# Constants of the graph convolution made inside its first layer instead of in a stage of their own

## The chip, the cores and the metric

One core of a Trainium2 chip runs one program. The metric is device microseconds from launch to end, and the median of several runs is what counts. The engines are TensorE (PE), VectorE (DVE), ScalarE (ACT), GpSimd (POOL) and SyncE (SP, which here only issues DMAs).

## The reference

`x` is 6250 nodes by 768, with 100000 edges plus a self loop for each node.

```python
x = x + gnn(_layernorm(x))        # two GCN layers, relu between them
x = x + ffn(_layernorm(x)[None])  # soft mixture of 32 experts with 32 slots each
# one GCN layer:  out = segment_sum((h @ W)[src] * dinv[src] * dinv[dst], dst) + b
# in the ffn:     phin = scale * phi / max(sqrt(sum(phi * phi, axis=0)), 1e-12)   (phi: 768 x 1024)
```

## The kernel before

The program runs five stages, each a block in which every engine has its own instruction list, with a barrier between them: `prepare` (layer norm, degrees, index tables, and a table of the node rows as a high and a low fp16 half in HBM), `constants`, `first_layer`, `second_layer` and `mixture`. All products are made with numbers split into two fp16 halves, so that a product takes three matmul passes (high by high, high by low, low by high).

`constants` loads W1, b1, W2, b2 and phi, finds power-of-two scales for W1 and W2 (largest absolute value, over the partitions by `partition_all_reduce` on POOL), computes a bound on the layer's output from sums of squares, splits W1 and W2 into halves (`W1s`, `W2s`), and normalises the columns of phi: squares, a sum over the rows by matmuls with ones, root, reciprocal, product, and again two halves (`phi_h`, `phi_l`).

`first_layer` goes over 49 blocks of 128 destination nodes. For each block POOL issues 17 indirect gathers of 128 rows (3072 bytes a row) into a ring of 17 buffers. It may run at most 17 gathers ahead of what PE has consumed (`consumed`). PE multiplies each gathered tile by a one-hot matrix (`pick`, made by DVE in `choose`) and sums in PSUM (`a_part`, L1021). The rest of a block is a chain over PE, DVE and ACT, laid between the sum steps of the next block: DVE adds the block's own rows and evicts the sum (L965, L967), ACT and DVE make its halves `v2`, PE turns them (L1009), ACT and DVE copy the turned halves to `vT` (L928, L984), PE multiplies by W1 (L1002), DVE and ACT make the hidden halves (L987 to L992), PE turns these, ACT and DVE copy them (L934, L994), PE multiplies by W2, ACT and DVE write the result's halves (L924, L975), and SP stores them. The engines take their work strictly in the order of the code, in which PE's loop reads

```python
if i >= 2: product(W2s)    # block i - 2
steps(0, 5);  turn(v2)     # block i - 1
steps(5, 9);  product(W1s) # block i - 1
steps(9, 14); turn(h2)     # block i - 1
steps(14, CT)
```

and DVE's, for block i: evict; low half of `v2`; low half of the stage of block i-1; `choose(i + 2)`; `add_own_rows(i + 1)` (L952, L954); copy to `vT` (L984); then bias, relu and halves, and the second copy.

## Time and the profile before

| | us |
|---|---|
| median of 3 runs | 3570.77 |
| lowest, highest | 3568.49, 3575.01 |
| the profiled execution, whole | 3575.02 |
| its span, first to last instruction | 3573.1 |
| PE busy in it | 3145.4 (88%) |
| DVE, ACT, POOL busy | 2003.8, 1196.0, 1860.2 |

The mean granted TensorE clock of the profiled execution is 0.972 of full speed. DMA moved 1016.48 MB, 284 GB/s on average. Times in the trace are microseconds from the start of its span. In a timeline row, the time in brackets is how long the engine was idle before the row, and what ended it.

### The profile page before, as it was taken

Reading aid. Unit: us, or ns where it says so; the run is one execution under the profiler, and the core shown is the slowest. Engines: PE = TensorE matmul, PEld = TensorE weight load, DVE = VectorE, ACT = ScalarE, POOL = GpSimd, SP = SyncE. Lnnn points to the kernel's source line nnn. Section 1 sums busy time; section 2 is a strip of 40 time slices with the busy share of each in tenths; the row PEclk is TensorE's granted clock in tenths of the full one; section 3 lists DMA queues with packets and bytes.
Section 4 is the critical chain, followed back from the end, with each engine's and each line's share of the span. In section 5 each row is a group of like instructions: output and inputs, shape, how many; then the busy total and the mean of one; then the engine's idle time right before and its main releaser. Section 6 shows DMA issues by size and latency. Waiting matters only on the chain. (4 is left out here: it accounts for less than half of the span.)

```text
span 3573.1 us, 60435 instructions
## 1 busy us (share of the span) xinstructions
PE 3145.4 (88%) x19503; PEld 2021.5 (57%) x19503; DVE 2003.8 (56%) x3053; ACT 1196.0 (33%) x1434; POOL 1860.2 (52%) x1757
## 2 busy tenths in 40 slices
PE   7214999999999999969999999999999985579998
PEld 6202666666666666635666666666666652235555
DVE  7865444444444444438888788887887872102422
ACT  6762222222222222215444444444444440111000
POOL 0104777777777777557666666666666620210000
PEclk9997999999999999989999999999999997789999
DMA  9374999999988999669888888888888848978975
GB/s 374 127 272 147 326 325 307 313 308 305 311 309 304 312 309 308 222 241 350 295 306 297 299 302 299 305 300 295 308 299 305 301 172 343 329 250 242 331 185 142
DMA packets 343943, 1016.48 MB, mean 284 GB/s; under 512 B 145058, under 2 KB 148924, under 8 KB 335472
## 3 DMA queue, kind: packets, MB, share of 16 engines
q0 software_dynamic: 139360, 696.24, 56.6%
q1 hardware_dynamic: 193252, 286.28, 23.9%
q10 hardware_dynamic: 11052, 30.21, 2.5%
q8 instruction: 179, 2.93, 0.3%
q14 instruction: 100, 0.82, 0.1%
HBM read 852.96 MB, written 133.90 MB: 276 GB/s over the span
## 5 line engine op out<-in xcount | busy, mean ns | idle before, releaser
L1194 POOL DMA_INDIRECT rows_mem<-table,idx x833 | 923.4, 1109 | 474.2 <-PE m_part L1373 235.3
L898 POOL DMA_INDIRECT rows_mem<-table,idx x833 | 883.1, 1060 | 347.2 <-issue 178.8
L1021 PE MATMUL a_part<-rows_mem,sums_mem 128*128 128x512 f16 (+1 forms) x3332 | 581.7, 328 | 48.1 <-DMA rows_mem<-table,idx 43.7
L1373 PE MATMUL m_part<-rows_mem,sums_mem 128*128 128x512 f16 (+1 forms) x3332 | 598.5, 329 | 28.7 <-DMA rows_mem<-table,idx 23.2
L1373 PEld LDWEIGHTS m_part<-rows_mem,sums_mem 128*128 128x128 f16 x3332 | 422.2, 142 | 171.2 <-issue 41.5
L1021 PEld LDWEIGHTS a_part<-rows_mem,sums_mem 128*128 128x128 f16 x3332 | 414.3, 142 | 176.7 <-issue 57.9
L1388 PE MATMUL m_ps_s<-m_dw,m_xn 128*128 128x512 f16 x1764 | 429.6, 380 | 32.3 <-DVE slots L1260 31.2
L1760 PE MATMUL e_po<-e_eh,e_cT 128*128 128x512 f16 (+1 forms) x1568 | 330.6, 331 | 67.1 <-DMA e_cT<-cw_dram 45.2
L1401 PE MATMUL m_ps_l<-phi_mem,m_xT 128*128 128x512 f16 x1764 | 388.7, 379 | 0.0
L1388 PEld LDWEIGHTS m_ps_s<-m_dw,m_xn 128*128 128x128 f16 x1764 | 210.3, 126 | 183.3 <-issue 57.8
L1401 PEld LDWEIGHTS m_ps_l<-phi_mem,m_xT 128*128 128x128 f16 x1764 | 172.5, 98 | 206.6 <-issue 0.2
L1760 PEld LDWEIGHTS e_po<-e_eh,e_cT 128*128 128x128 f16 x1568 | 152.7, 99 | 180.5 <-DMA e_cT<-cw_dram 47.8
L1002 PE MATMUL a_ps_o<-W2h,a_vT 128*128 128x512 f16 (+1 forms) x1176 | 248.4, 327 | 0.9 <-ACT a_vT L934 0.9
L1002 PE MATMUL a_ps_o<-W1h,a_vT 128*128 128x512 f16 (+1 forms) x1176 | 247.1, 326 | 2.0 <-DVE a_vT L984 2.0
L987 DVE SCALAR_TENSOR_TENSOR a_u<-a_ps_o,inv,brow 128x768 f32<-128x768 f32 x49 | 49.9, 1018 | 329.5 <-PE a_ps_o L1002 329.5
L1260 DVE TENSOR_TENSOR slots<-slots,m_ps_s 128x512 f32<-128x512 f32 x288 | 196.5, 684 | 42.4 <-PE m_ps_s L1388 41.8
L1200 ACT ACTIVATE m_part<-m_zeros 128x1536 f32<-128x1536 f32 x50 | 72.7, 1453 | 379.2 <-DVE sums_mem L1291 371.0
L1760 PE MATMUL e_po<-e_el,e_cT 128*128 128x512 f16 (+1 forms) x784 | 195.1, 331 | 0.0
L931 ACT ACTIVATE sums_mem<-a_u,dinv_s 128x768 f16<-128x768 f32 x49 | 45.9, 936 | 430.1 <-DVE a_u L987 430.1
L1002 PEld LDWEIGHTS a_ps_o<-W2h,a_vT 128*128 128x128 f16 x1176 | 115.4, 98 | 75.7 <-ACT a_vT L934 1.2
L1002 PEld LDWEIGHTS a_ps_o<-W1h,a_vT 128*128 128x128 f16 x1176 | 115.0, 98 | 76.0 <-ACT a_vT L928 2.1
L1002 PE MATMUL a_ps_o<-W2l,a_vT 128*128 128x512 f16 x588 | 144.3, 327 | 0.0
(357 smaller groups left out, 3930.1 us busy)
## 6 DMA issues: line engine op xcount, KB each, us to landing
sums_mem<-table SPq DMA_DIRECT2D x98, 384.0 KB, 6.0
rows_mem<-table,idx POOLq DMA_INDIRECT x1666, 5.2
cw_dram<-m_cst SPq DMA_DIRECT2D x49, 512.0 KB, 5.6
x_pad<-xs SPq DMA_DIRECT2D x7, 2688.0 KB, 23.9
table<-arena SPq DMA_DIRECT2D x49, 384.0 KB, 2.7
table<-a_stage SPq DMA_DIRECT2D x49, 384.0 KB, 4.2
sums_mem<-x_pad SPq DMA_DIRECT2D x49, 384.0 KB, 5.5
x_dram<-sums_mem SPq DMA_DIRECT2D x49, 384.0 KB, 4.2
```

The source lines that it names most:

```text
L898: pool.indirect_dma_start(out=ring[:, t, :], out_offset=None, in_=table, in_offset=bass.IndirectOffsetOnAxis(ap=idx[:, k:k + 1], axis=0)). ...
L931: nc.scalar.activation(h2[:, 0, :], u[:, :], ACT.Relu, scale=dinv_s2[:, bass.ds(b, 1)]).then_inc(h_hi, 1)
L987: v.scalar_tensor_tensor(u[:, :], ps_o[:, 0:D], inv[:, 0:1], brow[:, :], ALU.mult, ALU.add).then_inc(biased, 1)
L1002: mm = nc.tensor.matmul(ps_o[:, a:z], vT[:, half, c * P:(c + 1) * P], Wp[:, c, a:z], start=(c == 0 and half == 0 and Wp is Ws[0]), stop=(c ...
L1021: mm = nc.tensor.matmul(part[:, bass.ds(to + a, z - a)], pick[:, i % 2, :, t], ring[:, t, half * D + a:half * D + z], start=False, stop=(t ...
L1194: pool.indirect_dma_start(out=ring[:, t, :], out_offset=None, in_=table, in_offset=bass.IndirectOffsetOnAxis(ap=idx[:, n:n + 1], axis=0)). ...
L1200: nc.scalar.activation(part[:, :], zeros[:, :].to_broadcast([P, 3 * 512]), ACT.Copy).then_inc(wiped, 1)
L1260: v.tensor_tensor(slots[:, c, a:a + 512], slots[:, c, a:a + 512], ps_s[:, unit % 2, :], ALU.add).then_inc(added, 1)
L1373: mm = nc.tensor.matmul(part[:, bass.ds(off + at, e - f)], pick[:, i % 2, :, t], ring[:, n % RING, half * D + f:half * D + e], start=False ...
L1388: mm = nc.tensor.matmul(ps_s[:, u % 2, :], spread(xn[:, q % XN, xh, :], DC)[:, c, :], dw[:, q % DW, dh, a:a + 512], start=(q == bins[0] an ...
L1401: mm = nc.tensor.matmul(ps_l[:, a:a + 512], xT[:, half, c * P:(c + 1) * P], ph[:, c, a:a + 512], start=(c == 0 and half == 0 and ph is phi ...
L1760: mm = nc.tensor.matmul(ps_o[:, k % 2, a:e], cT[:, k % RT, half * HK + c, :], ee[:, HK * h + c, a:e], start=(c == 0 and half == 0 and ee i ...
```

## The change

`constants` and its barrier are gone, and what it did is spread over `first_layer`. The fp32 copies of W1, W2 and phi lie where they are free at that time (`slots`, `phi_mem`), and the squares of the weights in the place of W2's halves.

- SP issues W1, b1 and W2 right behind the load of block 0's own rows. phi, scale and b2 follow at its step 3, once W1's low half is made (`lo1`).
- POOL does the `partition_all_reduce` between gather 17 and gather 18.
- DVE runs `weight_scales` before block 0's eviction, `weight_halves` after it, `out_scales` in block 1, and W2's low half after block 0's copy to `vT`. ACT squares W1 and W2 and makes W1's high half before block 0, and W2's high half in it.
- The column sums of W2's squares are made by one DVE reduction over six chunks (`col_part`) and one ones-matmul, where 6 matmuls a column range did it before.
- phi's work is cut into parts of one 128x1024 chunk (a quarter of 1024 columns for the reciprocal), one part a block in `phi_parts`, on ACT and DVE from block 4 to block 29. PE gets one pair of 128x512 fp32 matmuls, at its step 12.

The core of the diff:

```diff
-                constants(nc, W1, b1, W2, b2, phi, scale, W1s, W2s, brow1, brow2, inv1, out2, dinv, dinv_s2, dinv_g,
-                          phi_h, phi_l, scl, slots, rows_mem, sums_mem, phi_mem)
...
+                    if i == 0:
+                        sp.dma_start(Wf1.rearrange("p (c d) -> p c d", c=DC), W1.rearrange("(c p) n -> p c n", p=P)).then_inc(w1_in, 16)
+                        sp.dma_start(brow[:, :], b1.rearrange("(o d) -> o d", o=1).to_broadcast([P, D])).then_inc(w1_in, 16)
+                        sp.dma_start(Wf2.rearrange("p (c d) -> p c d", c=DC), W2.rearrange("(c p) n -> p c n", p=P)).then_inc(w2_in, 16)
+                    if i == SQ_AT - 1:
+                        sp.wait_ge(lo1, 1)
+                        sp.dma_start(phi_f[:, :, :], phi.rearrange("(c p) e s -> p c (e s)", p=P)).then_inc(p_in, 16)
...
+                    if k == CT:
+                        pool.wait_ge(maxed, 2)
+                        pool.partition_all_reduce(wm[:, :], mx[:, :], P, bass.bass_isa.ReduceOp.max).then_inc(allmax, 1)
...
+                    v.tensor_reduce(u[:, :], sqw.rearrange("p (c d) -> p d c", c=DC), AX_X, ALU.add).then_inc(col_part, 1)
...
+                def weight_halves():
+                    v.wait_ge(f1_sum, 1)
+                    link(v.tensor_scalar(top2[:, :], ps_s[:, 0:1], 1.001 * D, None, ALU.mult))
+                    link(v.tensor_tensor(top2[:, :], top2[:, :], bsq[:, :], ALU.add))
+                    v.wait_ge(col_sum, 1)
+                    link(v.tensor_reduce(col[:, :], ps_o[:, 0:D], AX_X, ALU.max))
+                    link(v.scalar_tensor_tensor(top2[:, :], top2[:, :], 2.0, col[:, :], ALU.mult, ALU.mult))
+                    v.nop().then_inc(bound_r, 1)
+                    v.wait_ge(hi1, 1)
+                    v.scalar_tensor_tensor(flat(W1s[1]), Wf1, sc1[:, 0:1], flat(W1s[0]), ALU.mult, ALU.subtract).then_inc(lo1, 1)
...
+                def phi_parts(i):
+                    c = i - SQ_AT - 1
+                    if 1 <= c < DC:
+                        v.wait_ge(sqp_r, c + 1)
+                        wait(v, sqp_sum, c - 1)
+                        v.tensor_tensor(norm, norm, sq[c % 2], ALU.add).then_inc(sqp_sum, 1)
+                    if i == NORM_AT:
+                        v.wait_ge(rooted, 1)
+                        link(v.tensor_scalar(norm, norm, EPS_L2, None, ALU.max))
+                        link(v.tensor_scalar(scl[:, :], scl[:, :], 1.0 / (US * US), None, ALU.mult))
+                    c = i - RECIP_AT
+                    if 0 <= c < NR:
+                        part_n = norm[:, c * K // NR:(c + 1) * K // NR]
+                        link(v.reciprocal(part_n, part_n))
+                    c = i - UNIT_AT
+                    if 0 <= c < DC:
+                        v.tensor_tensor(phi_f[:, c, :], phi_f[:, c, :], norm, ALU.mult).then_inc(unit, 1)
+                    c = i - HIGH_AT - 1
+                    if 0 <= c < DC:
+                        v.wait_ge(unit, DC)
+                        v.wait_ge(hip, c + 1)
+                        v.scalar_tensor_tensor(phi_l[:, c, :], phi_f[:, c, :], US, phi_h[:, c, :], ALU.mult, ALU.subtract).then_inc(lop, 1)
...
                     if i + 1 < NBR:
                         add_own_rows(i + 1)
                     if i < NBR:
+                        phi_parts(i)
                         v.wait_ge(v_turned, i + 1)
                         wait(v, prod2, i)
                         v.tensor_copy(vT[:, 1, :], ps_t[:, 1, 0:D]).then_inc(vt_lo, 1)
+                        if i == 0:
+                            v.wait_ge(hi2, 1)
+                            v.scalar_tensor_tensor(flat(W2s[1]), Wf2, sc2[:, 0:1], flat(W2s[0]), ALU.mult, ALU.subtract).then_inc(lo2, 1)
```

`SQ_AT` is 4, `NORM_AT` 12, `RECIP_AT` 13, `UNIT_AT` 17 and `HIGH_AT` 23.

POOL's list, from the end of `prepare`, before the change (L728 is the reduction over the partitions, L898 a gather):

```order
L725 UNCONDITIONAL_BRANCH
L728 ISA
L728 ISA k_wm<-k_mx 128x2
L714 UNCONDITIONAL_BRANCH
L73 ISA
L893 UNCONDITIONAL_BRANCH
L898 DMA rows_mem<-table,idx 128x1536 x833
```

and with the change (L800 the reduction, L803 a gather):

```order
L795 UNCONDITIONAL_BRANCH
L803 DMA rows_mem<-table,idx 128x1536 x17
L800 ISA
L800 ISA a_wm<-a_mx 128x2
L803 DMA rows_mem<-table,idx 128x1536 x816
L769 UNCONDITIONAL_BRANCH
```

The reduction moved from its own stage to a place between two gathers.

DVE's list for block 0, from the low half of `v2` (L970) to the bias (L987), before the change:

```order
L970 SCALAR_TENSOR_TENSOR sums_mem<-sums_mem,dinv_as 128x768
L939 TENSOR_TENSOR sums_mem<-iota_x,dloc 128x2304
L820 TENSOR_LOAD tab
L820 ISA x2
L952 ISA
L952 TENSOR_TENSOR a_base<-sums_mem 128x768
L954 TENSOR_TENSOR a_base<-a_base,sums_mem 128x768
L984 COPY a_vT<-a_ps_t 128x768
L987 SCALAR_TENSOR_TENSOR a_u<-a_ps_o,inv,brow 128x768
```

and with the change, without the same five rows between L876 and L954 (L971 is the low half of `v2`, L908 and L993 the low halves of W1 and W2, L990 the copy, L996 the bias):

```order
L971 SCALAR_TENSOR_TENSOR sums_mem<-sums_mem,dinv_as 128x768
L901 TENSOR_SCALAR a_top<-a_ps_t 128x1
L902 TENSOR_TENSOR a_top<-a_top,a_bsq 128x1
L904 TENSOR_REDUCE a_col<-a_ps_o 128x1
L905 SCALAR_TENSOR_TENSOR a_top<-a_top,a_col 128x1
L908 SCALAR_TENSOR_TENSOR Ws<-slots,a_sc,Ws 128x4608
L876 TENSOR_TENSOR sums_mem<-iota_x,dloc 128x2304
...
L954 TENSOR_TENSOR a_base<-a_base,sums_mem 128x768
L990 COPY a_vT<-a_ps_t 128x768
L993 SCALAR_TENSOR_TENSOR Ws<-phi_mem,a_sc,Ws 128x4608
L996 SCALAR_TENSOR_TENSOR a_u<-a_ps_o,inv,brow 128x768
```

Four short operations and W1's low half now stand between the eviction and the copy to `vT`, and W2's low half between this copy and the bias.

DVE's list with the change in block 13, one of those with a part of phi's work:

```order
L980 SCALAR_TENSOR_TENSOR a_stage<-a_ps_o,out,a_stage 128x768
L876 TENSOR_TENSOR sums_mem<-iota_x,dloc 128x2304
L675 TENSOR_LOAD tab
L675 ISA x2
L952 ISA
L952 TENSOR_TENSOR a_base<-sums_mem 128x768
L954 TENSOR_TENSOR a_base<-a_base,sums_mem 128x768
L931 RECIPROCAL phi_mem<-phi_mem 128x256
L990 COPY a_vT<-a_ps_t 128x768
```

The reciprocal stands right ahead of the copy to `vT`. The other 21 parts stand at the same place, one in each of blocks 6 to 10, 12, 14 to 22 and 24 to 29.

## Rows read from the trace of the kernel before

**Rows 1.** Windows: busy time of each engine in the first layer's blocks 1 to 48.

```profile
core 0: us, PE busy (x) PEld busy (x) DVE busy (x) ACT busy (x) POOL busy (x), PEclk, DMA share, GB/s
360.00:1515.00 1155.00, 1151.32 (x7785) 798.36 (x7784) 504.35 (x570) 319.98 (x382) 844.39 (x799) 1.00 0.89 305
```

**Rows 2.** Timeline (start, duration, engine) of the constants stage, to the first layer's first instruction.

```profile
237.96 0.17 DVE L770 MEMSET k_ones<- 128x128 f32 x1 [5.32 <-PEq L74]
...
254.85 4.95 DVE L775 TENSOR_REDUCE k_mx<-rows_mem 128x1 f32<-128x4608 f32 x1 [1.13 <-DMA brow<-in_L_gnn_b_dram]
...
260.35 0.16 DVE L777 SCALAR_TENSOR_TENSOR k_bm<-k_wm,k_bm 128x1 f32<-128x1 f32 x1 [0.55 <-POOL k_wm L728]
...
263.71 0.25 DVE L783 TENSOR_SCALAR dinv_s<-dinv,k_sh 128x49 f32<-128x49 f32 x1
...
269.09 10.46 PE L743 MATMUL k_ps_n<-phi_mem,k_ones 128*128 128x512 f32 x24
...
272.00 5.02 DVE L793 SCALAR_TENSOR_TENSOR W1l<-rows_mem,k_sc,W1h 128x4608 f16<-128x4608 f32 x1 [1.48 <-ACT W1h L758]
...
281.87 0.15 DVE L664 TENSOR_SCALAR k_top<-k_top 128x1 f32<-128x1 f32 x1
...
283.20 0.25 DVE L800 TENSOR_SCALAR dinv_g<-dinv,k_invt 128x49 f32<-128x49 f32 x1
...
284.40 6.55 DVE L805 RECIPROCAL sums_mem<-sums_mem 128x1024 f32<-128x1024 f32 x1
290.99 6.56 DVE L806 TENSOR_TENSOR slots<-slots,sums_mem 128x6144 f32<-128x6144 f32 x1
...
310.45 0.06 DVE L942 MEMSET a_zeros<- 128x1 f32 x1 [0.88 <-PEq L74]
```

**Rows 3.** Timeline of the first layer's start, as far as block 0's first product.

```profile
311.49 39.38 SPq L883 DMA_DIRECT2D sums_mem<-table  x4
...
319.59 0.95 POOL L898 DMA_INDIRECT rows_mem<-table,idx  x1 [0.30 <-issue]
...
341.64 0.96 DVE L965 TENSOR_TENSOR sums_mem<-a_part,a_base 128x768 f32<-128x768 f32 x1 [23.43 <-PE a_part L1021]
...
345.29 5.15 PE L1021 MATMUL a_part<-rows_mem,sums_mem 128*128 128x512 f16 x20 [3.69 <-ACT a_part L905]
...
346.13 1.02 DVE L970 SCALAR_TENSOR_TENSOR sums_mem<-sums_mem,dinv_as 128x768 f16<-128x768 f32 x1 [2.67 <-ACT sums_mem L919]
...
353.55 0.49 PE L1002 MATMUL a_ps_o<-W1h,a_vT 128*128 128x512 f16 x2
```

**Rows 4.** DMA queues (packets, MB, share): 238 to 263, then 600 to 800.

```profile
q1 hardware_dynamic: 2784, 8.65, 91.3%
...
q0 software_dynamic: 11247, 55.29, 80.7%
```

**Rows 5.** Timeline of two later blocks, from `choose` to the product with W1.

```profile
641.22 1.35 DVE L939 TENSOR_TENSOR sums_mem<-iota_x,dloc 128x2304 f16<-128x2304 f16 x1
...
644.35 0.55 DVE L984 COPY a_vT<-a_ps_t 128x768 f16<-128x768 f16 x1
...
645.61 0.49 PE L1002 MATMUL a_ps_o<-W1h,a_vT 128*128 128x512 f16 x2
...
667.54 0.81 ACT L928 ACTIVATE a_vT<-a_ps_t 128x768 f16<-128x768 f16 x1 [3.02 <-PE a_ps_t L1009]
...
668.82 0.55 DVE L984 COPY a_vT<-a_ps_t 128x768 f16<-128x768 f16 x1
...
669.95 0.49 PE L1002 MATMUL a_ps_o<-W1h,a_vT 128*128 128x512 f16 x2
```

**Rows 6.** Timeline of the first layer's last block: two waits of PE.

```profile
1517.39 0.55 DVE L984 COPY a_vT<-a_ps_t 128x768 f16<-128x768 f16 x1
...
1518.04 0.49 PE L1002 MATMUL a_ps_o<-W1h,a_vT 128*128 128x512 f16 x2 [1.95 <-DVE a_vT L984]
...
1527.38 1.44 PE L1009 MATMUL a_ps_t<-ident,sums_mem 128*128 128x128 f16 x12 [3.33 <-DVE sums_mem L992]
```

**Rows 7.** Windows, columns as in rows 1: the stretch behind PE's second wait.

```profile
1527.00:1533.00 6.00, 4.72 (x23) 2.81 (x24) 0.79 (x2) 0.81 (x1) 0.00 (x0) 0.50 0.01 3
```

More of the change, by code:

```diff
@@ L668, in power_scale, with own_block, own_sum, donor_sum @@
     link(v.tensor_scalar(inv, pw, 1.0 / top, None, ALU.mult))
-def constants(nc, W1, b1, W2, b2, phi, scale, W1s, W2s, brow1, brow2, inv1, out2, dinv, dinv_s2, dinv_g, phi_h, phi_l, scl,
-              phi_f, rows_mem, sums_mem, phi_mem):
+def own_block(eng, tab, i):
+    w = eng.value_load(tab[0:1, 4 * i + 1:4 * i + 2], min_val=0, max_val=255)
+    return eng.snap(w & 63).with_bounds(min_val=0, max_val=NBR - 1)
+def own_sum(eng, tab, i):
+    w = eng.value_load(tab[0:1, 4 * i + 1:4 * i + 2], min_val=0, max_val=255)
+    return eng.snap(w >> 6).with_bounds(min_val=0, max_val=ACCS - 1)
+def donor_sum(eng, tab, i):
+    return eng.value_load(tab[0:1, 4 * i + 2:4 * i + 3], min_val=0, max_val=ACCS - 1)
+def pieces(mem, sizes):
+    at = 0
+    for n in sizes:
+        yield mem[:, at:at + n]
+        at += n
+def first_layer(nc, table, table2, W1, b1, W2, b2, phi, scale, Ws, brow, brow2, inv, out2, idx, dloc, tab, dinv, dinv_as, dinv_s2,
+                dinv_g, phi_h, phi_l, scl, phi_f, phi_mem, ident16, iota_x, rows_mem, sums_mem):
     with ExitStack() as ctx:
@@ L676, in sem @@
         def sem(name):
-            sems.append(nc.alloc_semaphore("k_" + name))
+            sems.append(nc.alloc_semaphore("a_" + name))
             return sems[-1]
         def sb(name, shape, dt):
-            return ctx.enter_context(nc.sbuf_tensor("k_" + name, shape, dt))
-        Wf1 = rows_mem[:, 0:2 * DC * D].bitcast(F32).rearrange("p (c d) -> p c d", c=DC)
-        Wf2 = rows_mem[:, 2 * DC * D:4 * DC * D].bitcast(F32).rearrange("p (c d) -> p c d", c=DC)
-        sqw = sums_mem[:, 0:DC * D].rearrange("p (c d) -> p c d", c=DC)
-        sqp = phi_mem[:, :].bitcast(F32).rearrange("p (c k) -> p c k", c=DC)
+            return ctx.enter_context(nc.sbuf_tensor("a_" + name, shape, dt))
+        acc, own, pick, tmp, v2, h2 = pieces(sums_mem, (ACCS * D, 2 * D, P * CW, D, D, D))
+        acc = acc.rearrange("p (a d) -> p a d", a=ACCS)
+        own = own.bitcast(F16).rearrange("p (s d) -> p s d", s=2)
+        pick = pick.bitcast(F16).rearrange("p (s n t) -> p s n t", s=2, t=CW)
+        v2 = v2.bitcast(F16).rearrange("p (h d) -> p h d", h=2)
+        h2 = h2.bitcast(F16).rearrange("p (h d) -> p h d", h=2)
+        ring = rows_mem[:, :].rearrange("p (t d) -> p t d", t=CT)
+        W1s = tuple(p.rearrange("p (c d) -> p c d", c=DC) for p in pieces(Ws, (DC * D, DC * D)))
+        W2s = tuple(p.rearrange("p (c d) -> p c d", c=DC) for p in pieces(Ws[:, 2 * DC * D:], (DC * D, DC * D)))
+        Wf1 = phi_f[:, :, :].rearrange("p c k -> p (c k)")[:, 0:DC * D]
+        Wf2 = phi_mem[:, 0:2 * DC * D].bitcast(F32)
+        sqw = Ws[:, 2 * DC * D:].bitcast(F32)
+        norm, sq0, sq1 = pieces(phi_mem[:, :].bitcast(F32), (K, K, K))
+        sq = (sq0, sq1)
+        SQ_AT = 4
+        NORM_AT = SQ_AT + DC + 2
+        RECIP_AT = NORM_AT + 1
+        NR = 4
+        UNIT_AT = RECIP_AT + NR
+        HIGH_AT = UNIT_AT + DC
+        assert HIGH_AT + DC + 1 < NBR
+        zeros = sb("zeros", [P, 1], F32)
         ones32 = sb("ones32", [P, P], F32)
@@ L1030, in _ @@
                         pe.wait_ge(biased, i - 1)
+                        if i == 2:
+                            pe.wait_ge(lo2, 1)
                         product(W2s).then_inc(prod2, 1)
+                    if i == NORM_AT:
+                        pe.wait_ge(sqp_sum, DC - 1)
+                        for at in (0, 512):
+                            mm = nc.tensor.matmul(ps_s[:, at:at + 512], ones32[:, :], norm[:, at:at + 512], start=True, stop=True)
+                        mm.then_inc(normed, 1)
                     if i < NBR:
@@ L1054, in _ @@
                     steps(14, CT)
+                    if i == 0:
+                        pe.wait_ge(ones, 1)
+                        pe.wait_ge(f1_r, 1)
+                        nc.tensor.matmul(ps_s[:, 0:1], ones32[:, :], f1[:, :], start=True, stop=True).then_inc(f1_sum, 1)
+                        pe.wait_ge(col_part, 1)
+                        for a, z in ((0, 512), (512, D)):
+                            mm = nc.tensor.matmul(ps_o[:, a:z], ones32[:, :], u[:, a:z], start=True, stop=True)
+                        mm.then_inc(col_sum, 1)
 def spread(rows, n):
```

215 lines of the change are left out of this document (79 added, 136 removed).

## The prediction, made before the changed kernel ran

> **What bounds the kernel now.** I read the windows first. From 360 to 1515 us the first layer runs its 48 later blocks, and PE is busy for 1151.3 of 1155 us, at a granted clock of 1.00 [rows 1]. PE is the bound there, and a block takes 24.3 us (two products with W1 start at 645.61 and 669.95 [rows 5]). So whatever makes PE wait in a block, or gives it work, lengthens the kernel by as much. DVE has 504 us of work in that stretch and ACT 320, so both look free. The share of busy time does not say when they must be done, and that is what this change turns on.
>
> Then the timeline of the constants stage. Its first instruction on DVE starts at 237.96 and the first layer's at 310.45 [rows 2]. In these **72.5 us** nothing of the layers moves. It is a serial stretch: weights in by 254.85, scales, halves, and at the end phi alone, 6.55 us of reciprocals and 6.56 us of products on DVE and as much again for its halves [rows 2].
>
> **What it removes.** All of the 72.5 us, barrier included, since the first layer's instructions now follow where the constants' did. The rest of the sum is what comes back. I count it in the first layer's own time, t = 0 at DVE's first memset.
>
> **Weights beside the first gathers.** Before, block 0's product with W1 starts at 353.55 - 310.45 = 43.1 [rows 3]. Now it has to wait for W1's low half, which hangs on the landing of W2 (T), since both largest values go through one reduction on POOL. Behind T, on DVE: 4.95 us for the largest value of W2, 0.55 until POOL has answered (260.35 - 259.80), 3.6 for the scales (260.35 to 263.96), the column sums. These are new: a reduction over 128x4608 with its inner step across chunks, which no row shows. The same number of elements takes 4.95 us in a straight reduction; I take that, and twice that as the upper bound. So far T + 14.1. Then block 0's eviction to the low half of `v2`, 5.5 us (341.64 to 347.15 [rows 3]), four short operations (1.6, with the maximum over 768 columns counted as the 0.96 us of L965), W1's low half 5.02 [rows 2], and `choose`, own rows and the copy 3.7 (641.22 to 644.90 [rows 5]), and 0.1 to PE's start. Together **T + 30.0**.
>
> PE would get there at T + 26: it may start block 1's sums 3.65 us after the eviction starts (345.29 against 341.64), and came to the product 8.3 us later [rows 3]. So PE waits 4 us here. ACT's pieces (squares, two high halves; at DVE's pace for as many elements 5 us each) end before DVE wants them. W2's low half (5.0 us) lies beside the product with W1 (18 passes of 768 columns, 5.8 us at 2.4 GHz) and is free; without that cover it would cost its 5.0.
>
> T itself: four loads on SP's queue (own rows, W1, b1, W2) are 5.5 MB, the same as W1, b1, W2, b2 before, which were in 16.9 us after the stage's start [rows 2]. SP's first load of the layer issues at 1.04 (311.49 [rows 3]), so alone T would be 18. But POOL's fourth gather issues at 9.1 and the others follow every 1.25 us (0.95 and 0.30 idle [rows 3]): 0.39 MB each, 314 GB/s asked, of the 380 that the loads alone reached (8.65 MB in 91.3% of 25 us [rows 4]). At 9 some 1.5 MB of the weights are in, 4.0 are left, and 5.9 MB of gathers. With an equal share of bytes, 190 GB/s each, T = 30. Packet by packet, a weight packet (3.1 KB, 131 ns) against a gather packet (4.9 KB, 230 ns; both from [rows 4], share times 16 engines times the stretch over packets), the weights get 138 GB/s until the gathers are done at 36, and T is about 36. I take **T = 32**, nearer the first, since the packet times of [rows 4] count gaps too. The bounds are 20 (weights first; then the gathers end block 0's sums late and nothing earlier helps) and 36.
>
> The Trainium skill ("DMA: Bandwidth & Descriptors", section "Queues, rings and completion order") says that each DMA engine takes turns between queues by the packet. By that the later T, 36, would hold, and the gain would be 4 us smaller. No row here has a bulk load and the gathers together.
>
> Block 0's product then starts at 62.0 against 43.1: **18.9 us back**. POOL stands between gather 17 and 18 until T + 5.5; 10 gathers would be out when PE starts block 1, at 1.25 us each, and PE sits in its wait meanwhile, so that costs nothing, nor would 4 us more for the first gather behind it.
>
> **The clock behind that wait.** After 3.33 us of waiting PE's granted clock is 0.50 of full speed, 1.2 GHz, for the next 6 us [rows 6, 7]; after 1.95 us it was not lowered: the product from 1518.04 has its two matmuls in 0.49 us, as at 645.61 [rows 5, 6]. The 4 us wait is of the first kind. In those 6 us PE was busy for 4.72, which is 2.36 at full speed: **2.4 us** (bounds 0 and 3).
>
> **`out_scales` in block 1.** Eight linked operations, 1.6 us (281.87 to 283.45 [rows 2]). ACT's and DVE's stage copies now wait for them, and the copy to `vT` comes up to 1.6 us later; less the slack of 0.55 (next part): **1.0 us**.
>
> **The parts of phi.** This is the term that the busy shares hide. In a steady block the copy to `vT` ends at 644.90 and PE starts the product at 645.61; one block later at 669.37 and 669.95 [rows 5]. These two gaps alternate over the blocks. When PE does wait for this copy, it starts 0.10 us behind it (1517.94 to 1518.04 [rows 6]). So DVE's slack is 0.61 or 0.48, **0.55 us** in the mean, with all 22 parts placed right ahead of that copy. Each is priced from [rows 2]: a product of 128x6144 takes 6.56, so one of 128x1024 1.23, and 0.09 of it overlaps with the next: 1.14. A quarter of the reciprocals: 6.4 / 4 + 0.15, and 0.04 for the link: 1.79. The 5 sums, 6 products, 6 low halves and the clamping (priced as these, somewhat shorter) are 18 times (1.14 - 0.55) = 10.7; the 4 reciprocals 4 times (1.79 - 0.55) = 5.0. **15.7 us.** ACT's parts come at the same place, but ACT idles 3.02 us ahead of its copy [rows 5] and a part is at most DVE's 1.2 us: free.
>
> **PE's own part.** 24 records of 128x512 fp32 matmuls in 10.46 us [rows 2] are 12 matmuls, so the two of step 12 cost **1.7 us**. The root on ACT (at most 1.2 us) ends before the turn that waits for it, behind five sum steps of 1536 columns, 3.2 us. phi's 3.5 MB run beside the gathers when the ring holds several tiles that PE has not reached; the gathers need 275 GB/s and would get 190 to 218 for 18 to 25 us, at most 1.5 MB or 4 tiles less than they need: free.
>
> **The sum.** 72.5 - 18.9 - 2.4 - 1.0 - 15.7 - 1.7 = **32.8 us** less. The profiled execution took 3575.0, 4.3 above the median, so it would be 3542.2, and against the median of 3570.8 it is **3538**.
>
> **Rivals.** (1) The parts hide after all: DVE's chain ahead of the copy could move forward, as each begins from ACT's stage copy and not from PE's end. Then 15.7 comes back: 3522. Against it, the gap of 0.58 to 0.71 comes out the same in block after block. (2) The start costs more: T at 36, column sums 5 us longer, the first gathers behind POOL's reduction late enough to starve block 1, phi's load felt. Some 17 us in all: 3555. What speaks for it is only that none of these has a row. (3) The other side: each of the 22 waits of 0.6 to 1.2 us lowers PE's clock as the 3.33 us one did. Each would then cost 2.4 more, 53 in all: 3591, slower. It decides from 1.5 us a wait on (32.8 / 22). Against it stands the wait of 1.95 us that lowered nothing [rows 6]. (4) No change: it needs 26 to 40 us more than summed, which (2) and a third of (3) together would give.
>
> **Chances.** The sum as it stands, within 8 us: 0.58. (1) 0.17, (2) 0.17, (3) 0.05, (4) 0.03. A difference under 0.2%, 7 us, could hardly be told from none on this kernel. So faster 0.92, same 0.03, slower 0.05. The range from 3518 to 3556 takes in (1) and (2) and leaves out the last two and the tails.
>
> **What would show it.** In the changed profile: the first gather near 238.6; W2's landing 32 us behind the first memset and the largest-value reduction there; column sums of 5 us; block 0's first product near 300 with a wait of about 4 us; 22 waits of PE for the copy to `vT`, 0.6 us at the tensor operations and 1.2 at the reciprocals; every block without a part again 24.3 us. It goes wrong if the slack ahead of the copy is not what it looks like, or if T is far off.

## The result, and the profile after

The kernel before took 3568.51 us in this measurement (median, 3566.08 to 3575.01) and the changed one **3545.78 us** (3543.81 to 3550.94). The ratio is 0.9932, with a 95% interval of 0.992 to 0.9943. That is 22.7 us less, where 32.8 were forecast, and the time lies in the forecast range. The profiled execution of the changed kernel took 3543.81 us, its span is 3541.9, and its mean granted clock 0.964.

The windows of the changed kernel over the stretch of [rows 1], and over six microseconds beside block 0's first product (busy time of each engine, number of instructions, granted clock, DMA share, GB/s):

```profile
core 0: us, PE busy (x) PEld busy (x) DVE busy (x) ACT busy (x) POOL busy (x), PEclk, DMA share, GB/s
360.00:1515.00 1155.00, 1128.08 (x7578) 774.60 (x7576) 516.93 (x576) 323.05 (x384) 802.33 (x762) 1.00 0.85 292
305.00:311.00 6.00, 6.00 (x23) 3.01 (x24) 4.82 (x1) 0.00 (x0) 5.39 (x3) 0.62 0.86 285
311.00:317.00 6.00, 5.92 (x42) 4.14 (x41) 2.60 (x3) 0.94 (x1) 4.78 (x5) 1.00 1.02 414
```

In the first row PE is busy for 23 us less than in [rows 1], since the window now reaches into the layer's tail (block 48's eviction, the step in which DVE takes the sum of a block out of PSUM, is at 1482.71) and since PE waits for the parts of phi. The second row shows the lowered clock behind a wait, 0.62 in the mean, and the third shows it back at 1.00.

The timeline of the start, with the steps of the forecast's chain in their order (start, duration, engine; in brackets the idle time before, and what ended it). In this timeline and those below, rows of other work are left out between the rows shown:

```profile
237.67 0.06 DVE L941 MEMSET a_zeros<- 128x1 f32 x1 [5.30 <-PEq L74]
238.30 0.94 POOL L803 DMA_INDIRECT rows_mem<-table,idx  x1 [55.40 <-POOLq L74]
258.62 4.95 DVE L883 TENSOR_REDUCE a_mx<-slots 128x1 f32<-128x4608 f32 x1 [13.06 <-DMA brow<-in_L_gnn_b_dram]
272.15 4.95 DVE L886 TENSOR_REDUCE a_mx<-phi_mem 128x1 f32<-128x4608 f32 x1 [7.72 <-DMA phi_mem<-in_L_gnn_W_dram]
277.24 0.37 POOL L800 PARTITION_ALL_REDUCE a_wm<-a_mx  x1 [17.10 <-DVE a_mx L886]
277.65 0.16 DVE L888 SCALAR_TENSOR_TENSOR a_bm<-a_wm,a_bm 128x1 f32<-128x1 f32 x1 [0.55 <-POOL a_wm L800]
281.28 7.99 DVE L897 TENSOR_REDUCE a_u<-Ws 128x768 f32<-128x4608 f32 x1
289.19 0.94 DVE L966 TENSOR_TENSOR sums_mem<-a_part,a_base 128x768 f32<-128x768 f32 x1
293.66 1.02 DVE L971 SCALAR_TENSOR_TENSOR sums_mem<-sums_mem,dinv_as 128x768 f16<-128x768 f32 x1 [2.67 <-ACT sums_mem L848]
296.29 5.02 DVE L908 SCALAR_TENSOR_TENSOR Ws<-slots,a_sc,Ws 128x4608 f16<-128x4608 f32 x1 [0.16 <-DVE a_top L905]
297.05 5.08 POOL L803 DMA_INDIRECT rows_mem<-table,idx  x1 [0.30 <-issue]
304.35 0.55 DVE L990 COPY a_vT<-a_ps_t 128x768 f16<-128x768 f16 x1
304.82 5.01 DVE L993 SCALAR_TENSOR_TENSOR Ws<-phi_mem,a_sc,Ws 128x4608 f16<-128x4608 f32 x1
305.00 8.24 PE L1011 MATMUL a_ps_o<-Ws,a_vT 128*128 128x512 f16 x36 [5.23 <-DVE a_vT L990]
...
1517.15 0.06 DVE L1292 MEMSET m_zeros<- 128x1 f32 x1 [4.03 <-PEq L74]
```

The layer starts at 237.67 against 310.45 [rows 2], 72.8 us earlier. Its end, the next stage's first memset, is at 1517.15 against 1543.41, 26.3 us earlier. So 46.5 us come back inside the layer. Behind it the two profiled executions still differ by 5.0 us (3575.02 - 3543.81 = 31.2 in all, less 26.3 to the ends of the layer), in stages that the change does not touch. Over the traces of the kernel before, the changed one and e1 to e4 below, the second layer differs by up to 4.2 us and the mixture by up to 3.6, so this is within the spread of single executions, and the reason why I work with the layer and the blocks below.

A block with a reciprocal of phi (block 13) and PE's product behind it:

```profile
627.60 0.96 DVE L954 TENSOR_TENSOR a_base<-a_base,sums_mem 128x768 f32<-128x768 f32 x1
628.47 1.74 DVE L931 RECIPROCAL phi_mem<-phi_mem 128x256 f32<-128x256 f32 x1
630.25 0.56 DVE L990 COPY a_vT<-a_ps_t 128x768 f16<-128x768 f16 x1
630.91 1.35 PE L1011 MATMUL a_ps_o<-Ws,a_vT 128*128 128x512 f16 x7 [1.14 <-issue]
```

The copy ends at 630.81 and PE starts 0.10 us behind it, 1.14 us late. The profile puts the wait down to "issue", since the copy had only just ended; the gap of 0.10 shows what PE waited for. All 22 blocks with a part of phi on DVE show this gap. In the blocks without one it is 0.58 or 0.71, as before, except at the layer's two ends (0.10 in blocks 0, 1 and 48, 1.56 in block 47) and in block 11, where PE has its own two matmuls (1.85).

The column of periods from one block's eviction to the next reads 24.34 us for the blocks without a part (one, block 36, has 24.62, for which nothing here gives a cause), 24.90 and 25.03 in turn for those with an operation over 128x1024 (25.27 in block 25), 25.69, 25.79, 25.68 and 25.56 for those with a reciprocal, 24.64 for the clamping, and 26.06 where PE has its own two matmuls.

### The profile page after: what moved, and what is told of

It is laid out like the page before. It is cut to its first block and busy times, and to the rows that moved or that the text cites. A ratio compares the mean times of both kernels' runs of the same rounds, so it can differ in the third digit from the quotient of the medians.

```text
span 3541.9 us, 60369 instructions
## 1 busy us (share of the span) xinstructions
PE 3139.1 (89%) x19463; PEld 2011.8 (57%) x19463; DVE 2018.4 (57%) x3072; ACT 1196.9 (34%) x1444; POOL 1860.7 (53%) x1757
## 5 line engine op out<-in xcount | busy, mean ns | idle before, releaser
L803 POOL DMA_INDIRECT rows_mem<-table,idx x833 | 885.0, 1062 | 378.3 <-issue 176.8
L1030 PE MATMUL a_part<-rows_mem,sums_mem 128*128 128x512 f16 (+1 forms) x3332 | 580.9, 328 | 64.6 <-DMA rows_mem<-table,idx 63.6
L1011 PE MATMUL a_ps_o<-Ws,a_vT 128*128 128x512 f16 x3528 | 594.0, 328 | 20.5 <-issue 12.2
L1011 PEld LDWEIGHTS a_ps_o<-Ws,a_vT 128*128 128x128 f16 x3528 | 344.4, 98 | 253.8 <-issue 29.3
L996 DVE SCALAR_TENSOR_TENSOR a_u<-a_ps_o,inv,brow 128x768 f32<-128x768 f32 x49 | 49.8, 1017 | 313.9 <-PE a_ps_o L1011 313.9
L971 DVE SCALAR_TENSOR_TENSOR sums_mem<-sums_mem,dinv_as 128x768 f16<-128x768 f32 x49 | 49.9, 1019 | 130.8 <-ACT sums_mem L848 130.8
L1318 DVE TENSOR_TENSOR sums_mem<-m_part,m_base 128x512 f32<-128x512 f32 x98 | 50.1, 553 | 114.8 <-issue 81.6
L810 ACT ACTIVATE a_part<-a_zeros 128x768 f32<-128x768 f32 x100 | 77.2, 804 | 99.2 <-DVE sums_mem L968 89.5
```

The costliest lines, as they stand in the source:

```text
L803: pool.indirect_dma_start(out=ring[:, t, :], out_offset=None, in_=table, in_offset=bass.IndirectOffsetOnAxis(ap=idx[:, k:k + 1], axis=0)). ...
L810: nc.scalar.activation(part[:, at:at + D], zeros[:, :].to_broadcast([P, D]), ACT.Copy).then_inc(wiped, 1)
L1011: mm = nc.tensor.matmul(ps_o[:, a:z], vT[:, half, c * P:(c + 1) * P], Wp[:, c, a:z], start=(c == 0 and half == 0 and Wp is Ws[0]), stop=(c ...
L1030: mm = nc.tensor.matmul(part[:, bass.ds(to + a, z - a)], pick[:, i % 2, :, t], ring[:, t, half * D + a:half * D + z], start=False, stop=(t ...
L1318: v.tensor_tensor(tmp[:, f:e], part[:, at:at + e - f], base[:, f:e], ALU.add).then_inc(scaled_u, 1)
```

## Experiments

"Own time" below is counted from the layer's first memset. For each kernel I read it at the same places (start, in us):

| kernel | product of block 0 | eviction of block 1 | eviction of block 48 |
|---|---|---|---|
| before | 43.09 | 55.26 | 1199.15 |
| changed | 67.33 | 81.72 | 1245.04 |
| e1, parts behind the copy | 67.40 | 81.14 | 1228.74 |
| e2, reciprocals whole | 67.21 | 81.10 | 1247.47 |
| e3, gathers wait | 67.74 | 86.88 | 1250.30 |
| e4, column sums on PE | 62.31 | 78.92 | 1242.66 |

The kernel before took 3573.05 us beside e1 to e4. The theory under test is the forecast's: PE is the bound, DVE has 0.55 us of slack at the copy to `vT`, and whatever stands ahead of that copy beyond it lengthens the block one for one.

**e1_parts_behind_copy.** `phi_parts(i)` is moved from ahead of the copy to behind it:

```diff
                     if i < NBR:
-                        phi_parts(i)
                         v.wait_ge(v_turned, i + 1)
                         wait(v, prod2, i)
                         v.tensor_copy(vT[:, 1, :], ps_t[:, 1, 0:D]).then_inc(vt_lo, 1)
...
                         if i == 0:
                             v.wait_ge(hi2, 1)
                             v.scalar_tensor_tensor(flat(W2s[1]), Wf2, sc2[:, 0:1], flat(W2s[0]), ALU.mult, ALU.subtract).then_inc(lo2, 1)
+                        phi_parts(i)
```

Expected:

> The changed kernel with DVE's part of phi's work one place later in each block: behind the copy to vT that the product with W1 waits for, ahead of the bias. Theory (the 22 waits come from the place of the parts on DVE, not from their amount): all 22 waits vanish, blocks with a part take 24.34 us again, and the first layer is 16.4 us shorter (the measured lengthening of the 22 blocks), so about 3529 us. DVE waits some 6 us at the new place, and the longest part is 1.8 us. Rival (the parts cost by amount, through DVE's memory traffic, semaphores or the matmuls' clock): the blocks stay longer than 24.34 us and the time stays near 3545.

Measured: **3531.41 us** (3528.45 to 3533.25), ratio 0.988, interval 0.9865 to 0.9896, which does not meet that of the changed kernel. Block 48's eviction comes 16.3 us earlier than in the changed kernel. The blocks with a part take 24.34 us, those with the clamping or a reciprocal 24.39 (one 24.67). Here is the clamping's block in the timeline:

```profile
599.22 0.96 DVE L954 TENSOR_TENSOR a_base<-a_base,sums_mem 128x768 f32<-128x768 f32 x1
600.10 0.55 DVE L989 COPY a_vT<-a_ps_t 128x768 f16<-128x768 f16 x1
600.57 0.68 DVE L926 TENSOR_SCALAR phi_mem<-phi_mem 128x1024 f32<-128x1024 f32 x1
...
601.36 6.01 PE L1011 MATMUL a_ps_o<-Ws,a_vT 128*128 128x512 f16 x36
...
607.47 1.02 DVE L996 SCALAR_TENSOR_TENSOR a_u<-a_ps_o,inv,brow 128x768 f32<-128x768 f32 x1 [6.03 <-PE a_ps_o L1011]
```

The part now lies beside the product, and DVE still idles for 6.03 us before it gets the product's sum. The same instructions, moved by one place in DVE's list, cost almost nothing: the 22 blocks are 0.8 us longer in all, where they were 16.5 longer. (0.6 of the 16.3 us lie before block 1's eviction, since block 0's product took 7.54 us in this execution and 8.24 in the changed kernel's.) So nearly all of it is the place and not the work.

**e2_recip_whole.** The four quarters of the reciprocals are one operation again, ahead of the copy:

```diff
-        NR = 4
+        NR = 1
```

> The changed kernel with the reciprocal of 1024 columns in one part (6.55 us) in one block in place of four parts of 1.79 us. Theory that a wait of PE beyond some 3 us also lowers the clock behind it, while the 22 short ones do not: one wait of about 6.0 us and a slow product behind it, 2.2 us more, together 8.2, against 5.4 for the four waits now: 2.8 us more than the changed kernel in the first layer. Rival (the clock behind the wait is not touched in mid-layer, the loss at block 0 is of the cold start): 0.6 us more. Rival two (each short wait already lowers the clock): 1.0 us or more less, as three waits are gone.

Measured: 3551.38 us (3543.99 to 3554.2), ratio 0.9934, interval 0.9919 to 0.9949. The one block takes 32.56 us, 8.2 more than 24.34, where the four quarters together cost 5.4. Block 48's eviction comes 2.4 us later than in the changed kernel (expected: 2.8); in the whole time so little can't be told. The timeline and the windows of this block:

```profile
628.58 6.54 DVE L931 RECIPROCAL phi_mem<-phi_mem 128x1024 f32<-128x1024 f32 x1
635.16 0.56 DVE L990 COPY a_vT<-a_ps_t 128x768 f16<-128x768 f16 x1
635.82 8.08 PE L1011 MATMUL a_ps_o<-Ws,a_vT 128*128 128x512 f16 x36 [5.95 <-issue]
```

```profile
635.80:642.00 6.20, 6.18 (x26) 3.08 (x27) 0.00 (x0) 0.00 (x0) 0.94 (x1) 0.66 0.63 241
642.00:648.00 6.00, 5.88 (x45) 4.24 (x44) 2.64 (x3) 0.94 (x1) 2.57 (x3) 1.00 0.24 60
```

PE waits 5.95 us, and then its product takes 8.08 us instead of 6.01 at a granted clock of 0.66. Both the length of the wait and the clock's price behind it are in the block's 8.2. The waits of 1.14 us in the changed kernel show no such price: the products behind them take 6.01 us. That is what rules the slower rival out.

**e3_gathers_wait.** POOL's gathers start only when the weights have landed, and the reduction over the partitions stands behind gather 4:

```diff
+                pool.wait_ge(w1_in, 32)
+                pool.wait_ge(w2_in, 16)
...
-                    if k == CT:
+                    if k == 4:
```

> The changed kernel, but POOL waits for W1, b1 and W2 to land before its first gather, and does the reduction over the partitions after gather 4 instead of 17. This takes the gathers away from beside the weights. Theory (the late landing of W2, 34.4 us into the stage, is the two loads sharing the DMA engines): W2 is in at 18 us, the 16 us are contention. Block 0's sums then end at about 49 us and its product with W1 starts near 64.6 us, against 67.3 now, so hardly earlier: what one load gains the other loses. Rival (W2 is late for another reason, the queue's latency or the placing in slots and phi_mem): W2 lands at 25 us or later.

3550.18 us in the one execution that there is, so nothing is said of its time. The landing is as expected. DVE's reduction over W2 starts at 18.58 us of own time instead of 34.48, so the gathers are what delays the weights by 16 us. The product is a miss: 67.74, where 64.6 was expected. POOL's and DVE's timeline shows why:

```profile
255.95 4.95 DVE L888 TENSOR_REDUCE a_mx<-phi_mem 128x1 f32<-128x4608 f32 x1 [0.16 <-DMA phi_mem<-in_L_gnn_W_dram]
256.67 0.94 POOL L805 DMA_INDIRECT rows_mem<-table,idx  x1 [74.01 <-DMA phi_mem<-in_L_gnn_W_dram]
...
260.40 0.94 POOL L805 DMA_INDIRECT rows_mem<-table,idx  x1 [0.30 <-issue]
267.75 0.37 POOL L802 PARTITION_ALL_REDUCE a_wm<-a_mx  x1 [6.40 <-issue]
268.15 0.16 DVE L890 SCALAR_TENSOR_TENSOR a_bm<-a_wm,a_bm 128x1 f32<-128x1 f32 x1 [7.25 <-POOL a_wm L802]
```

The reduction's input is there at 260.9 and the last gather has issued at 261.34, but it starts 6.40 us later. The gathers behind it, the block's sums and its eviction (at 51.8 us of own time, 49 expected) are late with it. In the changed kernel such a pause would lie inside the 17.10 us in which POOL waits for DVE, so nothing there shows it. The late gathers then put block 1's eviction at 86.88. Holding the gathers back buys an early scale and pays for it with late rows: no gain.

**e4_col_on_pe.** The column sums of W2's squares go back from DVE's reduction to 12 matmuls on PE:

```diff
-                    v.tensor_reduce(u[:, :], sqw.rearrange("p (c d) -> p d c", c=DC), AX_X, ALU.add).then_inc(col_part, 1)
...
-                            mm = nc.tensor.matmul(ps_o[:, a:z], ones32[:, :], u[:, a:z], start=True, stop=True)
+                            for c in range(DC):
+                                mm = nc.tensor.matmul(ps_o[:, a:z], ones32[:, :], sqw[:, c * D + a:c * D + z], start=(c == 0), stop=(c == DC - 1))
```

> The changed kernel with the column sums of W2's squares made on PE by 12 fp32 matmuls, as before the change, in place of DVE's reduction with the step across chunks (7.99 us in the changed kernel's trace, priced at 4.95 in the prediction) and 2 matmuls. PE is idle there. Theory (DVE's chain from W2's landing to W1's low half sets block 0's first product): the eviction of block 0 starts 8.0 us earlier and the product 8.0 us earlier, about 3538 us. Rival (PE's 12 matmuls, 10.4 us at the lower clock and begun 4 us after W2's landing, delay block 1's sums until they are the later arm): 3 to 5 us only.

Measured: 3545.84 us (3541.45 to 3546.55), ratio 0.9917, interval 0.9904 to 0.9931, which overlaps that of the changed kernel, so the time does not tell the two apart; the own times do. The product comes at 62.31 of own time, 5.0 us earlier and not 8.0, and of this 2.8 are left at block 1's eviction and 2.4 at block 48's. The timeline, PE, ACT, DVE and POOL:

```profile
276.11 10.50 PE L1082 MATMUL a_ps_o<-Ws,a_ones 128*128 128x512 f32 x24 [4.15 <-ACT Ws L835]
...
279.74 4.13 ACT L837 ACTIVATE Ws<-slots,a_sc 128x4608 f16<-128x4608 f32 x1 [3.69 <-DVEq L891]
...
284.77 0.95 DVE L966 TENSOR_TENSOR sums_mem<-sums_mem,a_part 128x768 f32 x1 [1.26 <-ACT sums_mem L843]
...
291.80 5.07 POOL L803 DMA_INDIRECT rows_mem<-table,idx  x1 [0.31 <-issue]
...
315.44 0.87 PE L1028 MATMUL a_part<-rows_mem,sums_mem 128*128 128x512 f16 x4 [0.87 <-DMA rows_mem<-table,idx]
```

With 8 us out of DVE's list, two things are late next. DVE waits for ACT, whose high half of W1 and zeroing fill 279.74 to 284.62 (the second has no row here). And PE now waits for gathers of block 1 (0.54 and 0.87 us), since POOL restarts behind the reduction as late as before and loses 8 us in two gather issues of 5 us (the other is at 300.30). A term of the start that looks like 8 us is worth 2 to 3 alone.

**The other chips.** The remaining eight kernels ran on three other chips. On these the kernel before takes 3803.0, 3826.54 and 3822.78 us, and in the traces of the eight kernels a block of the first layer takes 28.0 to 28.3 us in the median instead of 24.34. No trace of the kernel before was taken there. Only ratios to the kernel before on the same chip are compared there, and the expectations in microseconds don't apply as they stand. The edits: e5 is e1 and e4 together. e6, e8 and e12 are one kernel: the parts behind the copy, W1's scale with a partition reduction of its own 8 gathers ahead of W2's, the column sums in three DVE additions, W2's scale and halves behind block 0's copy:

```diff
+                    if k == CT:
+                        pool.wait_ge(maxed, 1)
+                        pool.partition_all_reduce(wm[:, 0:1], mx[:, 0:1], P, bass.bass_isa.ReduceOp.max).then_inc(allmax, 1)
+                    if k == CT + 8:
...
+                        pool.partition_all_reduce(wm[:, 1:2], mx[:, 1:2], P, bass.bass_isa.ReduceOp.max).then_inc(allmax, 1)
```

e7 and e9 are one kernel too. They keep `constants` for the weights and move only phi's part into the layer, with the parts ahead of the copy. e10 is the changed kernel, and e11 is e1, once more.

> The two edits together: DVE's parts of phi behind the copy to vT, and the column sums on PE. Theory (the two act at different places and add up): the first layer is 16.3 + 2.4 = 18.7 us shorter than in the changed kernel, evicting block 48 near 1226.4 us behind the layer's first instruction, and the time is 1 to 3 us below the first edit's alone, near 3529. Rival (the 2.4 us are only what the gathers' supply of block 1 leaves, and phi's load takes that back when the blocks are short): the same as the first edit alone, 3531.

> The first edit (parts behind the copy), and W1 taken ahead of W2: POOL reduces W1's largest value after gather 17 and W2's after gather 25, so that W1's scale and high half no longer wait for W2's landing; W2's largest value is found before block 0's eviction, its halves are made behind the copy to vT and behind the bias; the column sums are three contiguous additions on DVE (4.4 us in place of 8.0) between the eviction and the low half of v2. Theory (block 0's first product hangs on DVE's chain from W2's landing, and block 1 on POOL's restart): product of block 0 at 56 to 58 us behind the layer's first instruction (67.4 now), block 1's eviction 9 to 12 us earlier than in the changed kernel (81.7), about 3522. Rival (the gathers now run beside W2's load for longer and push its landing out by as much as they gain, and POOL pauses at each reduction): product at 62 or later, and 3527 or more.

> The kernel before with only phi's half of the change: the constants stage keeps the weights and loads phi, but phi's norms, products and halves are spread over the first layer's blocks 4 to 29 exactly as in the change. Theory (the sum by steps): the stage ends at about 284.5 instead of 310.4, 26 us less, and the blocks give back 16.4 + 1.7, so the gain is 8 us: 3561 beside 3569 before. The weights' half then makes the other 18 of the change. Rival (the halves are not additive, as PE's waits are shared or phi's blocks are lengthened by the late start of the gathers): a gain of 3 or of 20.

> The same kernel as the run with W1's scale made first, on another chip if it falls so. On a chip on which the kernel before takes about 3570 us, my theory gives: block 0's product at 57 to 59 us of the layer's own time instead of 67.3, block 1's eviction at 73 against 81.7, and every block with a part of phi at 24.34 us. The parts behind the copy gave 14.4 us in the median, the earlier start should add the 8.7 of block 1's eviction: 3522 us, ratio to the kernel before 0.986. Rival: the start's gain is given back later, as in the run with the column sums on PE: then 3531, as with the parts moved alone.

> The same kernel as the run with phi's part of the change alone (the weights stay in a stage of their own ahead of the layer). On a chip on which the kernel before takes about 3570 us, my theory gives: the layer starts 28 us earlier and gives back 16.4 us in the 22 parts and 1.7 in PE's own matmuls, 10 us in all: 3561, ratio 0.997. Rival: the parts hide, as they did on the slower chip: then 3545, ratio 0.993, and every block of 24.34 us.

> The changed kernel as it is, once more, beside the two better versions on one chip. On a chip with the pace of the first one: 3546 us, ratio 0.993. On the slower chip (3803 us for the kernel before) my theory is that the parts of phi cost nothing, since no block with a part was longer there: then this one gains about 45 us, ratio 0.988, and moving the parts adds nothing. Rival: the parts cost their 14 us there too: ratio 0.992.

> The kernel with the parts behind the copy, once more. On a chip of the first pace: 3531 us, 14 less than the changed kernel of the same call. On the slower chip, by my theory, the same time as the changed kernel of this call within 5 us; by the rival 14 less.

> The kernel with W1's scale made first and the parts behind the copy. On either chip block 1's eviction is 8.7 us earlier than with the parts moved alone; by my theory that comes through to the end, 9 us less than the kernel of the same call with the parts moved alone (3522 on a chip of the first pace). Rival: it is given back, and the two are equal.

| kernel | before there | median | ratio, interval | product of block 0 | eviction of block 1 |
|---|---|---|---|---|---|
| e5 | 3803.0 | 3759.43 | 0.9874 (0.985 to 0.9898) | 62.02 | 89.20 |
| e6 | 3803.0 | 3749.61 | 0.9865 (0.9843 to 0.9888) | 58.31 | 73.00 |
| e7 | 3803.0 | 3778.85 | 0.9938 (0.9916 to 0.9959) | | |
| e8 | 3826.54 | 3768.44 | 0.9853 (0.9828 to 0.9878) | 58.38 | 75.98 |
| e9 | 3826.54 | 3783.78 | 0.9875 (0.9854 to 0.9897) | | |
| e10 | 3822.78 | 3764.8 | 0.9845 (0.9824 to 0.9866) | 67.37 | 91.90 |
| e11 | 3822.78 | 3791.64 | 0.9906 (0.9889 to 0.9923) | 67.62 | 92.15 |
| e12 | 3822.78 | 3774.75 | 0.9878 (0.9861 to 0.9895) | 58.50 | 77.46 |

Most of the expected sizes failed here: e7 was to gain 8 us and gains 24, e9 10 and gains 43, e10 45 and gains 58, and e12 was to be 9 us faster than e11 and is 17. The product of block 0 came where it was expected in e8 (58.4, 57 to 59 expected) and just late in e6 (58.3, 56 to 58 expected).

What they show. First, the start: with W1's scale made first, block 0's product begins at 58.3 to 58.5 in three runs, 9 us earlier than in the changed kernel on any chip. Against e11, which shares the place of the parts, e12 is 16.9 us faster. At block 1's eviction it is 14.7 us ahead, so there the start is worth its time at the end.

Second, the parts. On the third chip e11 is 26.8 us *slower* than e10, against the 14 us gain of e1, and both my theory (equal) and its rival (14 faster) fail. e12, with its better start, is still 10 us slower than e10. The waits of PE from 500 to 1400 us on that chip, e10 first (in all, times, longest):

```profile
PE a_ps_t L1018 <- DVE sums_mem L1001: 64.5, 32, 2.7
PE a_ps_o L1011 <- issue: 17.4, 22, 1.7
```

and e11:

```profile
PE a_ps_o L1011 <- issue: 49.4, 28, 5.3
PE a_ps_t L1018 <- DVE sums_mem L1001: 34.4, 16, 3.4
```

On the first chip the same stretch holds 11.8 us of such waits in the changed kernel, 1.1 in e1 and none in the kernel before. Here PE waits in nearly every block, and not for the copy alone. The turn of the hidden halves comes late because DVE starts on the product's sum late, as in this block of e10:

```profile
704.57 6.01 PE L1011 MATMUL a_ps_o<-Ws,a_vT 128*128 128x512 f16 x36 [1.27 <-issue]
...
711.89 1.02 DVE L996 SCALAR_TENSOR_TENSOR a_u<-a_ps_o,inv,brow 128x768 f32<-128x768 f32 x1 [7.43 <-PE a_ps_o L1011]
...
715.45 0.83 PE L1018 MATMUL a_ps_t<-ident,sums_mem 128*128 128x128 f16 x12 [1.63 <-DVE sums_mem L1001]
```

DVE begins 1.31 us after the end that the profile gives the product. Over all 49 blocks the median of this lag is 1.96 us in e10 and 1.55 in e11, against 0.04 on the first chip. These ends are modelled, so either PE is slower there than its records say, or its signal comes later. Nothing here tells the two apart. The traces of these chips also give no time from issue to landing for the gathers (on the first chip it is 5 us), so a wait of PE for late rows could not be seen in them. The gathers' packets are hardly slower: 237 ns each in e10 and 231 in the changed kernel on the first chip, from 500 to 1400 us.

Where e11 loses can be read, though. Of its 49.4 us of waits, 46.1 lie ahead of the product with W2, up to 5.3 us at a time. This is block 6 of e11 (in brackets, "remote" means that the profile found no instruction that ended the wait):

```profile
491.09 0.83 PE L1018 MATMUL a_ps_t<-ident,sums_mem 128*128 128x128 f16 x12
...
498.25 0.56 DVE L1003 COPY a_vT<-a_ps_t 128x768 f16<-128x768 f16 x1 [7.30 <-remote]
499.11 8.12 PE L1011 MATMUL a_ps_o<-Ws,a_vT 128*128 128x512 f16 x36 [5.24 <-issue]
```

PE's turn of the hidden halves ends at 491.92 by its record, and DVE starts to copy them 6.3 us later. Waits of more than 1 us ahead of this product occur in all five kernels on these chips that have the parts behind the copy (38.5 to 46.1 us in all from 500 to 1400 us in e5, e6, e8, e11 and e12), apart from block 0 in blocks with a part alone. In e7, e9 and e10, with the parts ahead of the copy, they are 0.7 us or less, and in e1 on the first chip there are none. The products with W2 themselves take 337 us over the 49 blocks of e11 and 311 in e10. So on these chips the new place of the parts brings on waits at another product; by what mechanism stays open.

Third, phi's part alone (e7, e9) gains 24 and 43 us where the layer starts 27 to 28 us earlier than at 310.45 in the first chip's trace. The two differ by more than their intervals, so they settle nothing on whether the two halves of the change add up. In e7's trace the blocks with a part take 28.0 to 28.4 us like most of those without (in e9's both vary, from 24.8 to 29.8): where PE waits for something else anyway, the parts hide. So the 16 us of e1 were there to be gained only on the first chip.

## Why the prediction was right, and where it was off

The mechanism was right: serial time gone, a later first product, one lowered clock behind it, and 22 short waits. Of the 6.5 us that the gain at the layer's end falls short (26.3 against 32.8), 5.3 lie in one term. Predicted and measured, in the order of the forecast's sum:

| term | predicted | measured | from |
|---|---|---|---|
| removed | 72.5 | 72.8 | first memset, 310.45 and 237.67 |
| block 0's product later | 18.9 | 24.2 | own time 67.33 and 43.09 |
| clock behind that wait | 2.4 | 2.2 | 8.24 against 6.01 |
| `out_scales` | 1.0 | 0.9 | period 25.21 against 24.34 |
| 22 parts of phi | 15.7 | 16.5 | periods against 24.34 |
| PE's two matmuls | 1.7 | 1.7 | period 26.06 |
| left | 32.8 | 27.3 | 26.9 at block 48's eviction |

- **The failing term is the start**, "block 0's product then starts at 62.0 against 43.1", mis-sized by 5.3 us. W2 was in at 34.5 (predicted 32, bounds 20 and 36). The column sums were "4.95 us, and twice that as the upper bound": the row gives 7.99. These two are 2.5 and 3.0 us, in all 5.5, and both lie within the bounds that the forecast gave them. The rest of the chain held: T + 30.0 becomes T + 33.0 with the longer reduction, 67.5, and 67.33 was measured.
- **The landing.** The weights share with the gathers: without them they land at 18.6 (e3), with them at 34.5. That lies between the equal share of bytes (30) and turns by the packet (36). Which of the two holds is in the changed kernel's DMA queues from 250 to 262 us, where both have work (packets, MB, share):

```profile
q0 software_dynamic: 609, 2.97, 62.9%
q1 hardware_dynamic: 613, 1.78, 38.9%
```

  The gathers (q0) and the weights (q1) have the same number of packets and not of bytes; the weights get 148 GB/s, where 138 was worked out for turns by the packet and 190 for equal bytes. The forecast's choice of 32, "nearer the first", is the step that failed. The rule of the Trainium skill ("DMA: Bandwidth & Descriptors", section "Queues, rings and completion order") that each DMA engine takes turns between queues by the packet agrees with this case's trace. The reading that the fourth gather issues at 9.1 did not carry over either: in the kernel before the first two issues take 4.89 and 1.73 us, here 0.94 and 0.95, and the fourth starts at 4.4.
- **PE's wait** was predicted at 4 us and is 5.23, since PE's sums ahead of it took 6.9 us and not 8.3 (their first 20 matmuls 3.47 us against 5.15 in [rows 3]).
- **The clock** came out as foreseen, lowered after 5.23 and 5.95 us of waiting and not after 1.14, but the row that spoke against rival 3 was partly luck. The last block's product with W1 follows a wait of 1.95 us in all six traces of the first pace (before, changed, e1 to e4). It takes 6.01 us in four of them, the kernel before among them, and 7.69 in e1 and e4. The changed kernel first, then e4 (granted clock 1.00 and 0.78 over the product):

```profile
1491.14 6.01 PE L1011 MATMUL a_ps_o<-Ws,a_vT 128*128 128x512 f16 x36 [1.95 <-DVE a_vT L990]
...
1488.53 7.69 PE L1009 MATMUL a_ps_o<-Ws,a_vT 128*128 128x512 f16 x36 [1.95 <-DVE a_vT L988]
```

  On the other chips block 0's product takes 6.01 us behind waits of 2.68 and 2.97 (e6, e8) and 7.69 behind 2.77 and 2.82 (e11, e10). So behind waits of 2 to 3 us one execution says little about the clock. Behind the 22 waits of 0.14 to 1.15 us in the changed kernel it was lowered in no block.
- **The slack.** The reading that mattered most, that engines half idle still have 0.55 us of slack at one copy, is shown by e1: the parts' 16 us vanish when they are moved behind it. Its own numbers nearly hold: +0.57 or +0.70 for most tensor operations against 0.59 forecast, +0.30 for the clamping, +1.34 in the mean for a reciprocal against 1.24.
- **Rival 1** (the parts hide) fell by the 22 gaps of 0.10 us. **Rival 2** (a dearer start) was half true: T and the column sums, but neither the gathers behind POOL's reduction nor phi's load starved block 1 in the changed kernel. **Rival 3** (the clock lowered 22 times) fell: the products behind the short waits take 6.01 us. **Rival 4** would have needed all of rival 2 and a third of rival 3.
- Why the medians differ by 22.7 and the layer by 26.3: the interval of the ratio goes from 20.3 to 28.5 us, and holds both.
- All of this is for the first pace. On the third chip the same change gains 58 us (e10), for which the forecast has no row.

## What to carry to other kernels

Work that is to hide in an engine's idle time must stand where that engine waits, and not where it has merely less to do: find the instruction that the bounding engine waits for, measure the gap behind it over several blocks, and put the new work behind it. When a serial start is shortened, look up what is late next before counting the gain: here 8 us off one engine were worth 2 to 3. A placement tuned to slack below one microsecond holds for the chip that it was measured on: the better place of the first chip was the worse one on another, so the ratio should be taken on several. And where two loads share the DMA engines, count packets: here the bulk load and the gathers got equal numbers of packets, not equal bytes.
